# A decoder layer with a selective scan: Softplus as one activation, and eight diagonals of D kept in place of one

## The reference

```python
proj = jnp.einsum('blh,he->bel', x, W_in)               # 512 -> 2 * 1024
hidden, gate = jnp.split(proj, 2, axis=1)
hidden = silu(causal_conv4(hidden) + conv_bias)         # 1024 channels
dt, Bm, Cm = split(hidden^T @ W_x, [128, 144])          # 128, 16, 16
dts = jax.nn.softplus(dt @ W_dt + b_dt)                 # 512 x 1024
dA = jnp.exp(dts[..., None] * A)                        # x 16 states
dBu = dts[..., None] * Bm[:, :, None, :] * hidden[..., None]
state = dA * state + dBu                                # scan over 512 tokens
y = (sum_n(state * Cm) + hidden * D) * silu(gate)
x = layernorm(x + y @ W_out)
x = layernorm(x + xattn(x, ctx))
x = layernorm(x + int8_linear(x))
```

## Time and profile before

| | |
|---|---|
| median of 3 runs | 1209.81 us (1209.77 to 1210.84) |
| the profiled execution | 1212.85 us, of which the span of the trace is 1211.1 us |
| busy | DVE 80%, PE 72%, ACT 71%, POOL 67% |
| granted TensorE clock, mean | 0.856 of full speed |
| chain that ended last | PE 27%, issue 24%, ACT 18%, DVE 18%, DMA 5%, POOL 4% |
| DMA | 135.03 MB, mean 111 GB/s |

### The profile page before, as it was taken

How to read it: one execution, slowest core, us unless ns; L and a number is a source line. 1 busy time by engine, 2 the same in 40 slices (tenths; PEclk the granted TensorE clock), 3 DMA queues, 4 the chain that set the end, 5 groups by cost and what they waited for, 6 DMA issues and landing times.

```text
span 1211.1 us, 10560 instructions
## 1 busy us (share of the span) xinstructions
PE 866.9 (72%) x2718; PEld 339.3 (28%) x2718; DVE 974.8 (80%) x783; ACT 855.8 (71%) x1458; POOL 814.6 (67%) x515
## 2 busy tenths in 40 slices
PE   7933488878368789877549788896727946675995
PEld 2221133322023233332114233332202312222331
DVE  2459999987789987778888977887788999999733
ACT  2386777766557887786666886878756788787546
POOL 2238888876667776686767766868766777777533
PEclk9966699988679889988869899998977978778996
DMA  5184444442973334242793332443395353225100
GB/s 172 35 183 113 97 113 113 126 112 55 244 196 74 87 97 112 70 122 74 186 271 91 85 97 73 103 117 92 89 249 165 72 140 87 59 70 156 27 0 35
DMA packets 66684, 135.03 MB, mean 111 GB/s; under 512 B 13120, under 2 KB 19392, under 8 KB 66624
## 3 DMA queue, kind: packets, MB, share of 16 engines
q1 hardware_dynamic: 65904, 134.28, 43.5%
q10 hardware_dynamic: 720, 0.08, 0.0%
HBM read 62.75 MB, written 4.46 MB: 55 GB/s over the span
## 4 chain that ended last, share of the span: by engine, by line
PE 27%; issue 24%; ACT 18%; DVE 18%; DMA 5%; POOL 4%; SPq 2%; DVEq 0%; ACTq 0%; POOLq 0%
PE dense L919 18%; DVE st L817 12%; PE dense L974 6%; ACT dA L598 5%; POOL st L466 3%; DMA rep<-steps 2%; DVE dBu L811 2%; PE dense L951 2%; DMA wide<-w_out 1%; ACT squares L629 1%; DVE hs L795 1%; SPq L358 1%; ACT du_rep L606 1%; ACT tb L588 1%; PE dBu L929 1%
## 5 line engine op out<-in xcount | busy, mean ns | idle before, releaser
L466 POOL TENSOR_TENSOR st<-st,Cb 128x1024 f32<-128x1024 f32 x250 | 584.4, 2359 | 180.9 <-DVE st L817 153.5
L817 DVE TENSOR_TENSOR_SCAN st<-dA,dBu 128x1024 f32<-128x1024 f32 x256 | 570.2, 2269 | 0.3 <-ACT dA L598 0.3
L598 ACT ACTIVATE dA<-rep,Aneg 128x511 f32<-128x511 f32 x512 | 327.7, 710 | 82.0 <-DMA rep<-steps 51.6
L811 DVE TENSOR_TENSOR dBu<-du_rep,Bb 128x1024 f32<-128x1024 f32 x250 | 294.6, 1224 | 91.8 <-ACT du_rep L606 60.6
L919 PE MATMUL dense<-xTs,Win 128*128 128x512 f32 x512 | 242.2, 618 | 16.6 <-DMA xTs<-xT 7.7
L919 PE MATMUL dense<-wide,hs 128*128 128x512 f32 x256 | 122.2, 634 | 57.9 <-DVE hs L795 34.3
L919 PEld LDWEIGHTS dense<-xTs,Win 128*128 128x128 f32 x512 | 99.1, 198 | 154.2 <-issue 153.5
L974 PE MATMUL dense<-pj,Win 128*128 128x512 f32 (+1 forms) x192 | 106.1, 704 | 47.0 <-DVEq L798 21.2
L951 PE MATMUL dense<-st,sel 128*32 128x512 f32 x1024 | 124.3, 629 | 2.9 <-POOL st L466 2.9
L606 ACT COPY du_rep<-rep 128x512 f32<-128x512 f32 x128 | 74.4, 581 | 41.2 <-DVE dBu L811 39.4
L945 PE MATMUL dense<-hs,Ddiag 128*128 128x512 f32 x64 | 41.2, 731 | 81.9 <-ACT Ddiag L676 72.2
(11 more groups left out here) (117 smaller groups left out, 998.4 us busy)
## 6 DMA issues: line engine op xcount, KB each, us to landing
rep<-steps SPq DMA_DIRECT2D x512, 128.0 KB, 2.7
Win<-w_in SPq DMA_DIRECT2D x64, 256.0 KB, 2.7
wide<-w_out SPq DMA_DIRECT2D x4, 2048.0 KB, 14.0
Win<-w_conv SPq DMA_DIRECT2D x24, 256.0 KB, 2.7
wide<-bc_rows SPq DMA_DIRECT2D x24, 256.0 KB, 6.5
xTs<-xT SPq DMA_DIRECT2D x4, 1024.0 KB, 10.9
Bb<-bc_rows SPq DMA_DIRECT2D x16, 256.0 KB, 10.8
Cb<-bc_rows SPq DMA_DIRECT2D x16, 256.0 KB, 11.8
```

Source lines behind the costliest of these rows:

```text
L466: nc.gpsimd.tensor_tensor(s, s, C[:, j, :], ALU.mult).then_inc(s_p, 1)
L598: nc.scalar.activation(dA[:, u % 2, j, 1:T], rep[:, u % REPS, 0, 1:T], ACT.Exp, scale=Aneg[:, u % UNITS, j:j + 1]).then_inc(s_dA, 1)
L811: V.tensor_tensor(dBu[:, j, :], du_rep[:].unsqueeze(1).to_broadcast([P, JH, T]), B[:, j, :], ALU.mult).then_inc(s_mul, 1)
L817: V.tensor_tensor_scan(st[:, u % RING, j, :].rearrange("p j t -> p (j t)"), dA[:, u % 2, j, :].rearrange("p j t -> p (j t)"), dBu[:, j, :] ...
```

## The change

`soft` is one activation, Softplus of the product plus the bias, written to `steps` by ACT; POOL's addition L497 and its semaphore go. ACT now waits itself for the old contents of the `steps` slot to be used up, and frees the PSUM bank once the activation has ended. z leaves the list of those that take a pair of temporaries, and the ring has two pairs. `Ddiag` holds eight matrices, written by ACT at the start; the rewriting at g % 4 == 2 goes with its wait, and PE waits for `s_dd` only before the first y.

```diff
-TEMPS = 3
+TEMPS = 2
-DIAG_AT = 2
-    temp_keys = [key for key in order if key[0] in "zgc" or key[0] == "h" and key[1] == 0]
+    temp_keys = [key for key in order if key[0] in "gc" or key[0] == "h" and key[1] == 0]
-        Ddiag = sb("Ddiag", [P, P])
+        Ddiag = sb("Ddiag", [P, NE, P])
...
-                        pool.wait_ge(s_zw, 3 * (n + 1))
-                        if n >= 3:
-                            pool.wait_ge(s_dA, NJ * NQ * (n - 2))
-                        nc.gpsimd.tensor_tensor(steps[:, n % 3, 0, :], t, a, ALU.add).then_inc(s_dt, 1)
                         pool.wait_ge(s_dt, n + 1)
                         nc.gpsimd.tensor_tensor(steps[:, n % 3, 1, :], steps[:, n % 3, 0, :], hs[:, kb % 2, i, :],
                                                 ALU.mult).then_inc(s_du, 1)
-                        pool.sem_inc(s_temp, 1)
...
             def soft(b, e):
+                n = NE * b + e
                 ps, free = full(("z", b, e))
-                a, t = temp_slot(("z", b, e))
-                n = 3 * (NE * b + e)
-                nc.scalar.activation(t, ps, ACT.Abs, bias=bdt[:, e:e + 1]).then_inc(s_zw, 1)
-                nc.scalar.activation(a, ps, ACT.Relu, bias=bdt[:, e:e + 1]).then_inc(free, 1)
-                act.wait_ge(s_zw, n + 1)
-                nc.scalar.activation(t, t, ACT.Exp, scale=-1.0).then_inc(s_zw, 1)
-                act.wait_ge(s_zw, n + 2)
-                nc.scalar.activation(t, t, ACT.Ln, bias=ones[:, 0:1]).then_inc(s_zw, 1)
+                if n >= 3:
+                    act.wait_ge(s_dA, NJ * NQ * (n - 2))
+                    act.wait_ge(s_du, n - 2)
+                nc.scalar.activation(steps[:, n % 3, 0, :], ps, ACT.Softplus, bias=bdt[:, e:e + 1]).then_inc(s_dt, 1)
+                act.wait_ge(s_dt, n + 1)
+                act.sem_inc(free, 1)
...
+            act.wait_ge(s_masks, NMASKS)
+            for e in range(NE):
+                nc.scalar.activation(Ddiag[:, e, :], ident[:], ACT.Identity, scale=Dsk[:, e:e + 1]).then_inc(s_dd, 1)
...
-                n = NE * b + g // 4 - 1
-                if g % 4 == DIAG_AT and 0 <= n + 1 < NB * NE:
-                    if n + 1:
-                        product_done(act, ("y", n // NE, n % NE))
-                    nc.scalar.activation(Ddiag[:], ident[:], ACT.Identity, scale=Dsk[:, (n + 1) % NE:(n + 1) % NE + 1]
-                                         ).then_inc(s_dd, 1)
...
-                pe.wait_ge(s_dd, n + 1)
-                nc.tensor.matmul(ps, Ddiag[:], hs[:, b % 2, e, :], start=True, stop=False)
+                if n == 0:
+                    pe.wait_ge(s_dd, NE)
+                nc.tensor.matmul(ps, Ddiag[:, e, :], hs[:, b % 2, e, :], start=True, stop=False)
```

More of the change, by code:

```diff
@@ L248, in decoder_layer @@
         s_cc = sem("c_spread")
-        s_zw = sem("softplus_step")
         s_dt = sem("steps_ready")
```

## The result

| | before | the change |
|---|---|---|
| median | 1210.32 us of 4 runs (1209.77 to 1211.04) | 1175.43 us of 4 runs (1172.91 to 1177.77) |
| ratio | | 0.9711, 95% interval 0.9683 to 0.9739 |
| the profiled execution | 1212.85 us, span 1211.1 | 1177.67 us, span 1175.9 |
| granted TensorE clock, mean | 0.856 | 0.859 |

What follows compares the result with a forecast made beforehand. No engine is full; DVE waits in places for `du_rep` or PE products behind ACT's softplus and table loads. Seven terms sum to 31.8 us, taken from the 1209.81 us median: 1178.0 us, range 1167 to 1193.

Steps and rivals of the forecast that it cites:

- Softplus's price and place: On ACT at each z: one 1.283 us load and a 0.68 us Softplus; with its diagonal 2.1 us go.
- Start-up: Before DVE's first unit: the load falls in ACT's wait, 2.9 us gained; the eight diagonals hide in idle time.
- Batch 0's gates: Steps 10 to 23 of batch 0: each of four gates moves 0.7 us, then waits for POOL's pair; 2.8 us.
- Step 26: Batches 0, 1 and 2: DVE waits for `du_rep`, ACT has no gap before it; 2.1 us each, 6.3 us.
- Step 2: Batches 1, 2 and 3: load hidden in ACT's wait, DVE's waits limit the gain; 2.0 us each, 6.0 us.
- Step 10 of batch 3: DVE waited 2.12 us there and the diagonal stands in idle time; 1.8 us gained.
- Steps 10 and 14 of batches 1 and 2: Second convolution waited 0.88 us for `pj`, then PE's own queue bounds; 4 x 0.9 = 3.6 us.
- Steps 18 and 22 of batches 1 and 2: PE waited for `pj` and DVE for PE; the full 2.1 us at each place, 8.4 us.
- (a): Two pairs of temporaries bind in all twelve groups with convolutions: 14.8 us fewer gained, 1192.8 us; chance 0.14.
- (b): PE's queue is no bound at steps 10 and 14, gates find their pair: 10.4 us more, 1167.6 us; chance 0.05.
- (c): Softplus on ACT costs much more than other activations, deciding from 2.8 us; at 3.4 us, 1229 us; chance 0.04.
- (d): The change gives nothing; equally long chains lie beneath in PE's order and the transfers: 1209 us; chance 0.03.

Runs made afterwards that it cites:

- e0: The changed kernel run again as it is, beside the kernel before: 1177.17 us, ratio 0.9703.
- e1: The changed kernel with three pairs of temporaries and one diagonal rewritten for each block, so softplus's edit alone: 1175.5 us, ratio 0.9683.
- e8: The kernel before with only POOL's order changed, its product into hs ahead of the unit's products with C: 1193.95 us, ratio 0.9858.
- e5: The changed kernel with POOL's product into hs moved ahead of the unit's products with C: 1158.72 us, ratio 0.955.
- e7: The changed kernel with Softplus applied twice at each z, first in place in PSUM, then into steps: 1188.06 us, ratio 0.981.
- e6: The changed kernel with Relu in place of Softplus, leaving one table load of 63: 1159.5 us, ratio 0.9568.
- e2: The changed kernel with one diagonal rewritten for each block, still two pairs of temporaries: 1177.04 us, ratio 0.9705.
- e9: The changed kernel with three pairs, one rewritten diagonal, and POOL's product into hs ahead of the products with C: 1158.22 us, ratio 0.9564.

## Why the prediction held, point by point

**Softplus's price and place** were right. One load and 0.687 us (forecast 0.68), 1.98 us less of ACT at each z (forecast 2.1). ACT's busy time is 792.3 us, not "about 779": I had summed the lengths of the four activations, but each starts some 0.1 us before the one ahead of it has ended, and the page counts such an overlap once. I had also taken all 32 diagonals away, and eight stay.

**Start-up**, 2.9: 2.96 and 2.63 in the two executions of the changed kernel. That it looks exact is luck in the first. Over the ten profiled executions the first activation of the first `hs` block starts between 12.89 and 14.31 us, whichever kernel it is. Where it starts at 13.8 us or sooner ACT waits 2.56 us for PE at its copy of `dt_s`, where later 3.5 us. These are ACT's rows of the change, then of e0, the same kernel:

```profile
13.52 0.78 ACT L541 ACTIVATE ta<-dense,cb,ck 128x512 f32<-128x512 f32 x1 [2.69 <-PE dense L906]
54.95 0.59 ACT L601 COPY dt_s<-dBu 128x512 f32<-128x512 f32 x1 [2.56 <-PE dBu L916]
```
```profile
14.31 0.78 ACT L541 ACTIVATE ta<-dense,cb,ck 128x512 f32<-128x512 f32 x1 [3.32 <-PE dense L906]
56.68 0.58 ACT L601 COPY dt_s<-dBu 128x512 f32<-128x512 f32 x1 [3.50 <-PE dBu L916]
```

ACT idles 2.69 and 3.32 us behind the eight diagonals, so they are hidden, as forecast. Yet of the five executions with eight diagonals four were of the later kind, and of the five with one diagonal only one; I see no way from the diagonals to PE's first product, and ten executions do not settle it. It stays open, with up to 2 us at stake. e0 is of the same kind as the trace of before, so its 2.63 is the fair measure of the forecast. In the change's own execution ACT's small copy, which sends B and C off, started 5.18 us sooner (57.79 against 62.97), 1.65 of it by the kind, and then 1.9 us were lost again in one transfer. These are SP's issues of the store of B and C and of the first load of them:

```profile
58.40 0.34 SPq L386 DMA_DIRECT2D bc_rows<-small  x1
61.97 1.75 SPq L345 DMA_DIRECT2D Bb<-bc_rows  x4
```

They are 3.57 us apart, and 1.65 or 1.66 us in the nine other executions. The start-up term of a single execution is good to no better than 2 us.

**Batch 0's gates**, 2.8: 3.45 and 3.90. The step "the gate moves 0.7 us, not 2" was right where POOL is the bound, and the sum is near 2.8 partly by luck. Only two of the four gates waited for POOL, in the change by 1.80 and 2.36 us, where the same gates waited 1.56 for PE. The groups are 0.67, 0.39, 0.00 and 2.39 us shorter in one execution and 0.27, 0.69, 0.68 and 2.26 in the other; those that waited for POOL are the first and last of the one (0.67, 2.39) and the second and third of the other (0.69, 0.68). In the three with less than 0.6 the first hidden convolution on PE had become longer: 6.34 and 6.73 us where it was 5.29 and 5.36, and in e0 6.46 where it was 5.09. In the last group the second convolution took 3.66 us in both where it had taken 5.36: 1.7 us of that group's gain are TensorE's clock, of which more below. The third pair (e1) is worth 2.5 us there, not the 5.6 more that the full 2.1 in place of 0.7 in each of four groups makes: PE is the next bound.

**Step 26**, 6.3: 6.48 and 6.43. The size was right (1.7 to 2.8 us in each batch) and the reason was not whole. I had put "ACT works without a gap before it", which is true for the softplus, and missed that ahead of it ACT idled 11.5 us for the `dt` projection in batch 0, and some 7 in batches 1 and 2. Where that chain is mended, softplus's 2.1 us are worth nothing (e8 and e5 both 15.3). The row was in the trace of before, a group of 3 copies that waited 25.7 us for PE:

```profile
L610 ACT COPY dt_s<-dense 128x512 f32<-128x512 f32 x3 | 1.8, 586 | 25.7 <-PE dense L919 25.7
```

**Step 2**, 6.0: 4.11 and 6.32, so right in e0 and a third too much in the other; single places gave 1.16 to 2.41 us. **Step 10 of batch 3**, 1.8: 1.58. It held.

**Steps 10 and 14 of batches 1 and 2**, 3.6: 5.01 and 5.76. The 0.9 was read at step 15 alone and stood for both steps. At step 14 it gave 1.3 us in three cases of four (0.55 in the other). At step 10 it was the wrong wait: the second convolution had waited 0.05 us, and what DVE had to give was its wait for a product of the attention, of which 1.58 us went. DVE in batch 1, before and after:

```profile
423.86 0.69 DVE L885 TENSOR_REDUCE nmax<-dense 128x1 f32<-128x512 f32 x1 [2.12 <-PE dense L919]
```
```profile
409.72 0.69 DVE L872 TENSOR_REDUCE nmax<-dense 128x1 f32<-128x512 f32 x1 [0.54 <-PE dense L906]
```

**Steps 18 and 22 of batches 1 and 2**, 8.4: 11.85 and 11.86. Here each place gave more than ACT gave up, 3.42 and 3.14 us at step 18 and 2.71 and 2.58 at step 22. The failed step is "the full 2.1 each": a sum with PE's durations held fixed. They were not. This is PE at step 18 of batch 1, ahead of the second convolution and the convolution itself, before:

```profile
493.85 0.63 PE L937 MATMUL dense<-ident,small 128*128 128x128 f32 x4 [3.29 <-ACT ta L574]
494.94 5.22 PE L974 MATMUL dense<-pj,Win 128*128 128x512 f32 x8 [0.46 <-ACT pj L566]
```

after:

```profile
476.58 0.63 PE L924 MATMUL dense<-ident,small 128*128 128x128 f32 x4 [1.43 <-ACT ta L566]
477.67 3.66 PE L962 MATMUL dense<-pj,Win 128*128 128x512 f32 x8 [0.46 <-ACT pj L558]
```

in e7, in batch 1 and then at the same place of batch 2:

```profile
479.78 0.63 PE L927 MATMUL dense<-ident,small 128*128 128x128 f32 x4 [2.04 <-ACT ta L567]
480.87 5.36 PE L965 MATMUL dense<-pj,Win 128*128 128x512 f32 x8 [0.46 <-ACT pj L559]
```
```profile
758.64 0.63 PE L927 MATMUL dense<-ident,small 128*128 128x128 f32 x4 [2.05 <-ACT ta L567]
759.72 3.66 PE L965 MATMUL dense<-pj,Win 128*128 128x512 f32 x8 [0.46 <-ACT pj L559]
```

and in e6:

```profile
472.61 3.66 PE L962 MATMUL dense<-pj,Win 128*128 128x512 f32 x8
```

In batch 1 PE idled 3.29, 1.43, 2.04 and 0 us for ACT's `ta`, and the same eight products took 5.22, 3.66, 5.36 and 3.66 us. From before to after that is 1.86 us of idle time and 1.56 us of the products, together the 3.42 us of the place. The granted clock goes with the products' length; the windows of the whole group before and after:

```profile
489.06:506.29 17.23, 13.48 (x36) 6.24 (x35) 9.87 (x14) 12.95 (x20) 12.94 (x10) 0.90 0.23 62
```
```profile
473.66:487.46 13.80, 11.86 (x35) 5.60 (x35) 9.75 (x14) 10.89 (x18) 11.65 (x9) 1.00 0.29 77
```

The column behind POOL's is the granted clock: 0.90 before, with a part of the stretch at 1.2 GHz, and 1.00 after, all of it at 2.4 GHz. Over the eight products alone it is 0.70 before, 1.00 after and 0.68 in e7.

Where the clock falls is not settled by the idle time just ahead. In e7 PE idled 2.04 and 2.05 us at this place, and the products took 5.36 us in batch 1 and 3.66 in batch 2; e7's extra 0.69 us of ACT made its four groups of steps 18 and 22 longer by 2.4, 0.6, 0.7 and 2.0 us. e8 has a case without any Softplus: PE's second convolutions of steps 14 and 22 of batch 0 took 3.66 and 5.36 us before, and in e8, after the same 2.1 us of idle time,

```profile
189.59 5.36 PE L974 MATMUL dense<-pj,Win 128*128 128x512 f32 x8 [2.08 <-issue]
251.94 3.66 PE L974 MATMUL dense<-pj,Win 128*128 128x512 f32 x8 [2.09 <-issue]
```

so that one group lost 1.69 us and the other gained 1.69, and the table shows 0.00 for the two. That the four places of steps 18 and 22 gained more than 2.1 in both executions of the change, and in e1 and e2, says that it is no accident of one run; what set the clock at each place is open. Over the whole run the mean clock hardly moved (0.856 to 0.859).

**What counted at nothing.** PE's 72.2 us of waiting for the diagonal: right, e1 and e2 have 77.5 us and more of it and are no slower. POOL's additions: only the 0.7 us at batch 0's gates rest on them. The changes of batch: mostly right, with -0.24 and -2.79 us in all that is in no term. One place lost in both, 0.59 and 0.50 us at steps 22 to 25 of batch 3. That z's bank is now given back only when Softplus has ended would fit, and so would the 1.30 us that e7 lost there, but this was not tried.

**The rivals.** (a), the pairs bind in all twelve groups: no gate of batches 1 and 2 waited for POOL in the change, e0, e2 or e7. (b), neither bound binds: POOL and PE's longer convolutions did bind in batch 0; at steps 10 and 14 of batches 1 and 2 the gain of 1.3 to 1.6 us (once 0.55) lies between the 0.9 of the forecast and the 2.1 of this rival. (c), a slow Softplus: 0.687 us. At e7's 0.54 us per us a Softplus of 0.69 + 35 / (32 x 0.54) = 2.7 us would have used up the gain, an extrapolation, by a slope that is good to about 0.1, that agrees with the 2.8 of the prediction. (d), nothing: no. The Trainium skill ("ScalarE: Activation LUTs", section on table sets) asks to batch calls by set, and that was the rule set aside for the sum: the kernel before had a load ahead of Ln at each z and 65 in all, the change has 63, so Exp and Ln had shared none, and the 6.1 us of gain which the rule would have left did not come true. What the rule is after is real: e6 prices the loads that remain at 17 us of the time, 0.27 us each and not 1.283.

Not tried were the eight diagonals with three pairs, in this kernel or in the one before: they don't fit in SBUF together, which is why the change gives up a pair. What they are worth is known from e0 against e2, and e5 against e9 (with the third pair), alone.

## What to carry to other kernels

A place on an engine's path gives what the next late chain leaves, so look one chain further than the wait that ends last: here ACT's softplus was worth half its time, and a product that stood in the wrong order on POOL, which no busy share names, was worth 17 us by one move. Price the same microsecond in steps (take it away, add it, take more away): the slopes 0.54, 0.55 and 0.21 told where ACT stops to be the bound. Where TensorE waits for the engine that you relieve, the length of its own products may change too, here by up to 1.7 us for eight of them between the kernel before and the change, and in either direction, so a sum with fixed durations is off by that at each such place. And look at the gain place by place: two of the seven terms, the start-up and batch 0's gates, came out near by parts that the forecast did not have and that cancel.

## What was not expected of the hardware

- Eight products of 128x512 took 3.66 us at one place and 5.2 to 5.4 us at the same place in another run, with the granted clock over them at 1.00 and at 0.68 to 0.70. The idle time of PE just ahead does not tell which: after 2.04 and 2.05 us of it both lengths were seen in one run (e7). A change of 0.7 us on ACT moved one group by 2.4 us and its fellow in the next batch by 0.7.
- One Softplus over 128x512 from PSUM takes 0.687 us, where Abs with the same operands took 0.676, and the next load starts 0.16 us after its end where the program waits for it; Ln before was followed at once.
- The start-up came in two kinds, some 1.7 us apart at the copy of `dt_s`, along with when PE's first product was ready.
- The first load of B and C was issued 3.57 us after the store that it needs in one execution, and 1.65 or 1.66 us after it in nine.
